# Loads of tile numbers on TensorE: one of 18 or 27 numbers against several of 6 or 9

## The reference

```
edge_index = stack([src, dst])
x = layernorm(x + L0(x))   # mean of x[src] over the edges of a dst node, @ W_l.T, + x @ W_r.T + b_r
x = layernorm(x + L1(x))   # attention with 4 heads: softmax over the edges of a node; norm, relu
x = layernorm(x + L2(x))   # per edge: relu([x_i, x_j - x_i] @ W1 + b1) @ W2 + b2, mean over the edges
x = layernorm(x + L3(x))   # attention weights of edge n for node n
return x
```

## Time and profile before

| what | value |
|---|---|
| median of three timed runs | 542.7 us |
| the runs | 538.05, 543.71, 542.7 us |
| span of the profiled execution, first to last instruction | 537.2 us |
| mean granted TensorE clock | 0.891 |
| PE / DVE / ACT / POOL busy | 428.4 / 385.2 / 288.1 / 229.8 us |
| chain that ended last | PE 65%, DVE 12%, issue 10% |

### The profile page before, as it was taken

One profiled execution on the slowest core, in us unless ns is written; L12 is line 12 of the kernel. 1 busy time (PEld: TensorE's weight loads), 2 busy tenths in 40 slices (PEclk: granted clock), 3 DMA queues, 4 the chain that ended last, 5 costly groups with the idle time before them and its releaser, 6 DMA issues.

```text
span 537.2 us, 8979 instructions
## 1 busy us (share of the span) xinstructions
PE 428.4 (80%) x2119; PEld 306.3 (57%) x2120; DVE 385.2 (72%) x992; ACT 288.1 (54%) x754; POOL 229.8 (43%) x221
## 2 busy tenths in 40 slices
PE   4986785699947676797799898998989989969820
PEld 2533443366823332345578686886868868748620
DVE  3477866657669986636689797896987969954434
ACT  0276855541584561135567676675776857742310
POOL 4610000021074660006667677575775757726040
PEclk8789988899976687897999999998998989998985
DMA  7600000000000000035557577575675756620001
GB/s 175 188 2 1 0 0 0 1 1 1 0 2 0 1 2 0 6 113 157 159 159 206 166 205 207 150 205 153 200 209 151 205 166 191 204 80 0 2 1 48
DMA packets 20440, 49.91 MB, mean 93 GB/s; under 512 B 4404, under 2 KB 8654, under 8 KB 20415
## 3 DMA queue, kind: packets, MB, share of 16 engines
q0 software_dynamic: 13120, 42.49, 27.3%
q1 hardware_dynamic: 6120, 5.95, 4.1%
q10 hardware_dynamic: 1174, 1.16, 0.8%
HBM read 47.66 MB, written 1.93 MB: 92 GB/s over the span
## 4 chain that ended last, share of the span: by engine, by line
PE 65%; DVE 12%; issue 10%; ACT 6%; DMA 4%; POOL 1%; ACTq 0%; DVEq 0%; POOLq 0%
PE ps L973 61%; DVE q_sb L798 3%; DMA w_lr<-in_L_gnn_W_r 2%; ACT arena L438 2%; PE ps L1187 2%; DVE x L779 2%; ACT arena L448 1%; DVE stats L723 1%; POOL al_g L390 1%; DMA arena<-q_table,gidx 1%; ACT xT L403 1%; PE ps L987 1%; ACT arena L403 1%; PE ps L1251 1%; DMA al_table<-al_sb 1%
## 5 line engine op out<-in xcount | busy, mean ns | idle before, releaser
L361 POOL DMA_INDIRECT arena<-q_table,gidx x162 | 157.1, 970 | 118.0 <-DMA q_table<-q_sb 44.3
L882 DVE TENSOR_TENSOR arena<-arena,ps 128x512 f32<-128x512 f32 x162 | 110.5, 682 | 33.8 <-PE ps L973 30.2
L973 PE MATMUL ps<-whole,hot 128*128 128x256 f32 x324 | 109.3, 420 | 16.9 <-issue 16.9
L973 PE MATMUL ps<-parts,hotT 125*128 x324 | 106.3, 411 | 1.4 <-issue 0.8
L973 PE MATMUL ps<-rounded,hot 128*128 128x256 f32 x324 | 96.3, 379 | 0.8 <-DVE rounded L888 0.8
L553 ACT ACTIVATE whole<-arena 128x256 f32<-128x256 f32 x162 | 67.7, 418 | 36.0 <-DVE arena L882 27.5
L973 PE MATMUL ps<-arena 128*128 128x512 f16 (+1 forms) x334 | 57.9, 333 | 24.1 <-issue 21.3
L973 PEld LDWEIGHTS ps<-whole,hot 128*128 128x128 f32 x324 | 51.3, 199 | 34.3 <-issue 20.6
L973 PEld LDWEIGHTS ps<-rounded,hot 128*128 128x128 f32 x324 | 63.0, 196 | 12.0 <-issue 3.0
L888 DVE SCALAR_TENSOR_TENSOR rounded<-arena,rounded 128x256 fp32r<-128x256 f32 x162 | 68.1, 420 | 0.6 <-ACT rounded L556 0.5
L556 ACT ACTIVATE rounded<-arena 128x256 fp32r<-128x256 f32 x162 | 66.3, 409 | 0.0
(11 more groups left out here) (182 smaller groups left out, 562.3 us busy)
## 6 DMA issues: line engine op xcount, KB each, us to landing
arena<-q_table,gidx POOLq DMA_INDIRECT x162, 3.6
q_table<-q_sb SPq DMA_DIRECT2D x5, 250.0 KB
w_sb<-in_L_gnn_W SPq DMA_DIRECT2D x1, 1024.0 KB, 11.8
x<-in_x ACTq DMA_DIRECT2D x1, 625.0 KB
out<-x SPq DMA_DIRECT2D x5, 125.0 KB
w_sb<-in_L_gnn_W SPq DMA_DIRECT2D x1, 512.0 KB, 12.1
arena<-in_dst SPq DMA_DIRECT2D x1, 312.5 KB
w_lr<-in_L_gnn_W_l ACTq DMA_DIRECT2D x1, 256.0 KB, 7.0
```

Of the source, the lines that this page charges most:

```text
L361: pool.indirect_dma_start(ring[:, k, :], None, q_dram[:, :], bass.IndirectOffsetOnAxis(ap=gidx[:, k:k + 1], axis=0)).then_inc(gathered[k], 16)
L882: V.tensor_tensor(ring[:, k, :], ring[:, k, :], ps[:, 5 + k % 2, :], ALU.add).then_inc(summed[k], 1)
L973: return nc.tensor.matmul(o, a, b, start=start, stop=stop, skip_group_check=True)
```

## The change

In the count stage the load of 18 numbers at the head of a turn is replaced by three loads of 6, one ahead of each group's waits. In the edge stage's loop the load of 27 numbers at the head of a pass is replaced by a load of 9 at the head of each of its four turns. The loops, the order of the products and all waits stay. Turns 1, 2 and 27 of the edge stage keep their loads of 9. The engines other than TensorE have the same instructions.

```
             def adjacency(g):
-                tiles = tiles_at(WIDE * g + (PAD - WIDE), WIDE)
                 for j in range(GROUPS):
+                    tiles = tiles_at(WIDE * g + (PAD - WIDE + GROUP * j), GROUP)
                     pe.wait_ge(src_built[j], g)
                     pe.wait_ge(dst_built[j], g)
                     for k in range(GROUP * j, GROUP * (j + 1)):
-                        mm(ps[:, bass.ds(tiles[k], 1), :], hot_dst[:, k, :], hot_src[:, k, 0:512], False, True)
-                        last = mm(flat[:, bass.ds(tiles[k] * 128 + 2560, 128)], hot_dst[:, k, :], hot_src[:, k, 512:NW],
+                        mm(ps[:, bass.ds(tiles[k - GROUP * j], 1), :], hot_dst[:, k, :], hot_src[:, k, 0:512], False, True)
+                        last = mm(flat[:, bass.ds(tiles[k - GROUP * j] * 128 + 2560, 128)], hot_dst[:, k, :], hot_src[:, k, 512:NW],
                                   False, True)
                     last.then_inc(hots_used[j], 1)
...
-            def pe_turn(g, first=False, last=False, tiles=None):
-                tiles = tiles or tiles_at(U * g - U, PAD + U + 1)
+            def pe_turn(g, first=False, last=False):
+                tiles = tiles_at(U * g - U, PAD + U + 1)
...
                 with pe.Fori(start, last, TOGETHER) as g:
-                    tiles = tiles_at(U * g - U, PAD + TOGETHER * U + 1)
                     for j in range(TOGETHER):
-                        pe_turn(g + j, tiles=tiles[U * j:])
+                        pe_turn(g + j)
```

## The result

The changed kernel takes 568.54 us (median of 4 runs, 567.33 to 569.32), the kernel before beside it 542.12 (538.05 to 543.71). The ratio is 1.0488, 95% interval 1.0443 to 1.0532: **slower by 26.4 us**, where 566 in a range of 555 to 575 was forecast. The span of the profiled execution is 567.6 us, 30.4 more than before. A span lies 1.7 us under its run's time here. So the profiled execution of the kernel before would have a time of 538.9, which is 3.2 us under that kernel's median, and the profiled one of the changed kernel, 569.32, lies 0.8 above its median. These make the 4 us between 30.4 and 26.4.

A forecast was written before the change was run, and what follows sets the result against it. The prediction took TensorE's sequencer, which issues nothing while it loads tile numbers, as the bound. Count stage +6.6, edge stage +16.3 and clock 0 gave +22.9 us; on the median of 542.7 that is 566, range 555 to 575.

The forecast's parts named there:

- Prices: Sequencer's loads: cheap from a multiple of four words, slow two words behind one; count stage's loads +3.5 us in sum.
- whole fours and single numbers: Fast loads: 0.08 us fixed, 0.265 for each whole four, 0.234 for each number left over; six numbers 0.81 us.
- an even price: Alternative fit for fast loads: 0.08 us fixed and 0.084 for each number; six numbers 0.59 us.
- Overhead of a load: Count stage: each of 18 extra loads brings a register operation with gaps, 0.13, and 0.05 us behind it; +3.2 us.
- Count stage: Paced by TensorE's sequencer alone: loads +3.5, overhead +3.2, ended waits for ACT -0.1; +6.6 us.
- the step that the clock costs nothing there: Count stage: a slow clock adds no time, since the sequencer sets the pace at both clocks.
- Stalls of the edge stage: Turns 3 to 26: twelve even turns 22.1, six odd 3.1, six pass heads 5.7 us; 30.9 against 14.6, +16.3.
- The clock: Edge stage: a third of twelve new stalls followed by slow stretches, as many as now; 0, between -5.6 and +11.2 us.

The follow-up runs named there:

- the runs with good addresses: Loads starting at multiples of four words: kernel before, count stage only, median 585.3 against 593.1 us; changed kernel's splitting, 592.9 against 593.1, once more ratio 0.9856.
- the first and the third set: Two sets of follow-up runs on other chips, in which the unchanged kernel before took 592.2 and 596.4 us.
- the edge half: Kernel before with only the edge stage's loads split, count stage as before: ratio 1.0163, once more 1.0053; without its gathers, on a 542.5 us chip, 1.0405.
- the loads of four: Kernel before with seven loads of four numbers spread over each edge-stage pass in place of one of 27, count stage as it was: ratio 0.9953.

## Why the prediction was right

Its mechanism held: the sequencer's loads are the "issue" stalls, they cost by their start, six and nine numbers are too few to hide, and each extra seam exposes its load. The sizes held less well: two misses of the count stage cancel, and the edge stage cost 6 us more than forecast. By its terms:

- **Prices.** Six numbers: 1.48 and 0.81 forecast, 1.48 and 0.82 measured (1.476 median, 0.815 shortest). The choice of whole fours and single numbers over an even price, 0.59, was right, and the 0.335 us for four confirms it a second time. Sum of the count stage's loads +3.5 forecast, +3.6 measured (31.4 against 27.8).
- **Overhead of a load**, 0.18 us forecast. In the changed kernel a later turn of the count stage takes 6.03 us without its loads, 5.70 before, which is 0.17 for each extra load; the runs with good addresses gave 0.19.
- **Count stage**, +6.6 forecast, +5.5 in the two profiled executions. The forecast priced the sequencer alone. From the first load to its last branch it took 108.5 - 29.5 = 79.0 us before and 118.5 - 31.7 = 86.8 after: +7.8, of which 3.6 are loads and some 3.0 overhead. Another 1.4 or so the prediction had put at nothing: the first load is over after 1.5 us instead of 4.3, and the sequencer then waits for the first one-hot matrices, which the long load had hidden. The first products after:

```profile
34.84 1.87 PE L973 MATMUL ps<-arena 128*128 128x512 f16 x12 [0.89 <-ACT arena L448]
```

  In the other direction went the step that the clock costs nothing there. Before the change the last turn, behind a 4.7 us stall at the slow clock, ran its products over 103.42 to 111.2 us, where 5.3 us would do at full clock, and the end of the stage waits for TensorE and not for the sequencer:

```profile
111.24 0.38 PE L973 MATMUL ps<-zeros 128*128 128x512 f16 x1
```

  TensorE ended 2.7 us behind the sequencer's last branch there and 0.4 behind it after. That +6.6 came near +5.5 is in part luck.
- **Stalls of the edge stage**, +16.3 forecast. By the chain after they are 30.9 us in turns 3 to 26 (twelve sum to 22.3, six to 3.0, six to 5.6), against 30.9 forecast and 14.6 before: +16.3.
- **The clock**, 0 forecast, between -5.6 and +11.2. The granted clock fell to half behind six of the twelve long stalls; before the change it did so behind four of the loop's stalls. That is some +2.8 at 1.40 each. Two of them, as busy time by stretch (the third number from the end is the granted clock):

```profile
323.20:326.60 3.40, 3.40 (x13) 2.74 (x10) 2.30 (x6) 1.61 (x6) 0.69 (x2) 0.51 0.56 177
360.80:364.00 3.20, 3.20 (x12) 2.61 (x10) 2.20 (x5) 1.51 (x5) 0.47 (x2) 0.50 0.58 165
```

- **A term that was missing.** 22.3 - 16.3 - 2.8 leaves 3.2 us. And the first pass of the trace before, at full clock, was itself 1.4 us longer than the second, with a late gather in its chain and a wait of 0.7 us of TensorE for `rounded`, which the trace after hasn't:

```profile
274.31 4.78 DMA arena<-q_table,gidx
```

  So up to 4.6 us are to be explained. Behind every stall the first six products take 1.40 us instead of 1.19, as the chain after shows at 266.14 and 267.60, and as the earlier trace rows showed at 257.87 for the trace before. Eighteen stalls more at 0.2 are 3.6 us. I counted a stall by its idle time alone, and left out that the products behind it are slower too. This is read from the traces; no run isolates it, and about 1 us stays open.

The median, 568.5, is within 3 us of 566 although the stage sums were 22.9 forecast and 28 measured. The forecast was added to the median of before, 542.7, while the execution whose stages are compared was some 3 us faster than that median and the one after 0.8 slower than its own; that too is luck. On the chips of the first and the third set the edge half gave +10 and +3 us only, the second not to be told from none; a trace from one chip doesn't warn of that.

## What to carry to other kernels

A load of registers by an engine's sequencer belongs to the path whenever the engine holds less work than the load lasts. Splitting it moves the stall without shrinking it and adds one exposure for each piece; by these numbers it can pay only if a piece, with its overhead, fits under the work in hand; the loads of four, 3 us less alone, are the one sign of that here. Look first at the address from which it loads: here a start at a multiple of four words instead of two behind one made it 1.8 times cheaper for six numbers and 2.7 times for 27, and a stride of 20 words for 18 numbers took 14.3 us off a stage of 81.7. And a wait that is the bound on one chip may cost half or less on another, so stage lengths tell more than whole times.

## What the runs showed of the hardware

- A TENSOR_LOAD on TensorE's sequencer from a multiple of four words takes 0.335 us for four numbers, 0.82 for six, 0.85 for nine, 1.59 for eighteen and 2.35 for twenty-seven; from two words off it takes 1.48, 2.18, 4.28 and 6.4 us. The first kind fits 0.08 fixed, 0.265 for each whole four and 0.234 for each number left over, the second 0.08 and 0.234 for each number, all within about 0.03 us. The Trainium skill ("Runtime: NRT & Kernel Launch", Instruction fetch mechanics) gives some 200 ns for each register, in bulk too, in a passage on loads from HBM; these loads are from SBUF. The trace comes near it for the second kind of start only, with 234 ns a number, and has about 85 in the first kind.
- The same skill ("DMA: Bandwidth & Descriptors", Latency and other measured facts) puts a floor of about 600 ns under a `tensor_load`; the runs here have 0.332 us for four numbers.
- In the edge stage the first products behind a stall took 0.2 us longer at full clock, 1.40 against 1.19 for six.
- The same kernel took 542 us on some chips and 592 to 596 on others; by the traces of its variants nearly all of the difference lies in one stage in which four engines exchange semaphores for every item.
